# A decoder layer on one core: a new order of the first stage, weights split in halves at other places, and causal tiles that share a bank

## The reference

```
x = x + self_attention(norm(x))       # 16 heads of 32, no mask, biases on q, k, v and output
x = x + cross_attention(norm(x), ctx) # q from x; k, v from 512 latent rows of 128; causal mask
x = x + gelu(norm(x) @ p1.T + b1) @ p2.T + b2   # 2048 hidden columns
```

## Time and profile before

| | |
|---|---|
| median of 3 runs | 1316.46 us (1315.13 to 1318.9) |
| the profiled execution | 1320.07 us, of which the span of its instructions 1318.3 |
| PE busy | 1226.2 us (93%), mean granted clock 0.956 |
| DVE, ACT, POOL busy | 705.5, 468.2, 439.4 us |
| chain that ended last | PE 70%, DVE 10%, POOL 8%, DMA 4%, issue 4%, ACT 3% |

### The profile page before, as it was taken

How to read it: one execution, slowest core, us unless ns; L and a number is a source line. 1 busy time by engine, 2 the same in 40 slices (tenths; PEclk the granted TensorE clock), 3 DMA queues, 4 the chain that set the end, 5 groups by cost and what they waited for, 6 DMA issues and landing times.

```text
span 1318.3 us, 16151 instructions
## 1 busy us (share of the span) xinstructions
PE 1226.2 (93%) x6176; PEld 807.4 (61%) x6176; DVE 705.5 (54%) x1078; ACT 468.2 (36%) x832; POOL 439.4 (33%) x410
## 2 busy tenths in 40 slices
PE   3889999999999887999999999899999999999998
PEld 2644566466556533565565565455678788788786
DVE  5556667766665755566666666554344421422322
ACT  3135544444553344435435345333412111111111
POOL 5034642633464356624425425535310100100000
PEclk9798999999999978999999999975999999999999
DMA  7442222443223333325334434422032000000000
GB/s 287 124 132 77 84 80 81 106 134 81 80 80 104 104 104 104 96 81 161 95 87 139 119 88 131 136 72 80 1 95 73 33 0 1 32 0 0 32 0 32
DMA packets 42711, 110.31 MB, mean 84 GB/s; under 512 B 5520, under 2 KB 10640, under 8 KB 36496
## 3 DMA queue, kind: packets, MB, share of 16 engines
q1 hardware_dynamic: 39840, 101.99, 26.7%
q0 software_dynamic: 2080, 6.82, 1.7%
q10 hardware_dynamic: 720, 0.54, 0.1%
HBM read 71.58 MB, written 37.75 MB: 83 GB/s over the span
## 4 chain that ended last, share of the span: by engine, by line
PE 70%; DVE 10%; POOL 8%; DMA 4%; issue 4%; ACT 3%; SPq 1%; DVEq 0%; ACTq 0%; POOLq 0%
PE PS L741 14%; PE PS L742 14%; PE PS L743 14%; PE PS L859 9%; PE PS L828 7%; PE PS L845 7%; DVE m_cols L1066 5%; POOL P_sum L547 3%; DMA stackK<-scratch 2%; POOL oTL L538 2%; DMA scratch<-stage 2%; PE PS L854 1%; ACT PT L666 1%; DVE PT L1029 1%; PE PS L831 1%
## 5 line engine op out<-in xcount | busy, mean ns | idle before, releaser
L1066 DVE TENSOR_REDUCE m_cols<-PS 128x1 f32<-128x512 f32 (+3 forms) x512 | 292.9, 588 | 206.6 <-PE PS L828 102.1
L666 ACT ACTIVATE PT<-PS 128x512 f32<-128x512 f32 (+3 forms) x512 | 250.9, 516 | 216.9 <-PE PS L848 99.6
L547 POOL TENSOR_TENSOR P_sum<-PT 128x512 f32<-128x512 f32 x128 | 161.1, 1280 | 346.6 <-ACT PT L666 346.4
L828 PE MATMUL PS<-stackK,stackQ 96*128 96x512 f32 (+3 forms) x512 | 215.2, 438 | 22.0 <-DVE m_cols L1066 15.6
L845 PE MATMUL PS<-stackQ,stackK 100*128 100x512 f32 (+3 forms) x512 | 203.1, 422 | 16.5 <-ACT PT L666 15.9
L828 PEld LDWEIGHTS PS<-stackK,stackQ 96*128 96x128 f32 x512 | 105.4, 208 | 103.4 <-DVE m_cols L1066 71.4
L845 PEld LDWEIGHTS PS<-stackQ,stackK 100*128 100x128 f32 x512 | 101.3, 201 | 97.1 <-ACT PT L666 44.0
L1150 DVE CAST hidH<-hid 128x512 fp32r<-128x512 f32 x64 | 30.6, 478 | 223.3 <-ACT hid L713 221.2
L713 ACT ACTIVATE hid<-PS,b1c 128x512 f32<-128x512 f32 x64 | 43.9, 687 | 277.1 <-PE PS L743 275.2
L1073 DVE RECIPROCAL P_sum<-PS 128x512 f32<-128x512 f32 x32 | 107.4, 3358 | 58.9 <-PE PS L859 58.9
L552 POOL TENSOR_TENSOR P_sum<-P_sum,PT 128x512 f32<-128x512 f32 (+1 forms) x128 | 125.0, 1005 | 8.0 <-ACT PT L666 4.3
(11 more groups left out here) (110 smaller groups left out, 1757.9 us busy)
## 6 DMA issues: line engine op xcount, KB each, us to landing
scratch<-stage SPq DMA_DIRECT2D x128, 256.0 KB, 7.5
...
```

The lines of the kernel that those rows point to most:

```text
L547: pool.tensor_tensor(P_sum[:, h, :], PT[:, h, :], PT[:, 4 + h, :], ALU.add).then_inc(p_added, 1)
L666: nc.scalar.activation(PT[:, (4 * k + h) % 8, q0:SEQ], PS[:, T_BANK + h % 2, q0:SEQ], ACT.Exp, scale=SCALE).then_inc(p_ready, 1)
L828: mm = nc.tensor.matmul(dst[:, 0:n], stackQ[0:STACK, par, h, q * P:(q + 1) * P], stackK[0:STACK, par, h, 0:n], start=True, stop=not cross)
L1066: nc.vector.tensor_reduce(m_cols[:, q, STACK + h:STACK + h + 1], PS[:, S_BANK + q % 2, 0:keys(u, q)], AX.X, ALU.max).then_inc(s_done, 1)
```

## The change

It has four parts.

1. **First stage.** The first sequence of x is loaded in two halves, the other three as three transfers behind the stack loads of units 0 and 1 (before: one of 3 MB ahead of them). POOL makes `ident` first and the constants for the stacks later; the low parts of WQ and WO move from DVE to POOL. DVE makes its four norms in a row. The maxima of unit 0 and the pieces of K of unit 1, V tiles 2 and 3, Q and K of unit 2 form a "unit -1", whose order comes from places:

```diff
+def first_order():
+    pieces = [(what, which, k) for what, which in (("K", 1), ("V", 2), ("V", 3), ("Q", 2), ("K", 2)) for k in range(KT)]
+    work = spread(pieces[:-AFTER_TURN], *FIRST_PIECES) + [(19.0, item) for item in pieces[-AFTER_TURN:]]
+    work = [(place, *item) for place, item in work] + [(17.0, "turn", 0, 0)]
+    work += [(float(j), "max", j, 0) for j in range(len(S_FILLS[SELF]))]
```

2. **Raw tiles.** Every raw tile is 512 columns wide (a chunk is two), has its half of the buffer in turn, and a place of its own. The first two loads are issued at the end of unit 11. POOL does the tiles with a place under 3 ahead of the adds of k = 1, from 3 to 9 ahead of those of k = 2, the others behind them:

```diff
         for k in range(KT):
-            RAW.append((12, [wq2T[k * P:(k + 1) * P, :]], (WQ2, k), ("V", BATCH - 1, KT - 1)))
+            weight(FIRST_RAW, (0.7, 2.0, 8.0, 8.8)[k], wq2T[k * P:(k + 1) * P, :], WQ2, k, ("V", BATCH - 1, KT - 1))
...
+            weight(FIRST_RAW, (19.0, 20.5)[k], wkv2T[:, k * DIM:(k + 1) * DIM], WKV2, k, Q_LAST)
...
+            weight(FIRST_RAW + max(k, 1), (10.0, 14.0, 14.0, 14.0)[k], wo2T[k * P:(k + 1) * P, :], WO2, k, K_LAST)
...
+CHUNK_PLACES = [(25, (10.0, 12.0)), (26, (10.0, 12.0)), (28, (7.0, 10.0)), (28, (16.0, 20.0)), (29, (10.0, 12.0)),
+                (30, (10.0, 12.0))]
```

3. **Causal tiles.** In cross units tiles share a bank: of the scores, the two heads of a pair at k = 2 and all four at k = 3; of the tiles for maxima, all four heads at q = 0 and two at q = 1. Each head keeps its own matmul; the mask's matmul, the exponential or the maximum is one for all. Of 16 banks filled in a unit 11 are left, on either side. The adds of k = 2 take two heads at once:

```diff
+T_FILLS = {SELF: [(k, h, 1) for k in range(KT) for h in range(HPG)],
+           CROSS: [(k, h, heads) for k, heads in ((0, 1), (1, 1), (2, 2), (3, 4)) for h in range(0, HPG, heads)]}
+S_FILLS = {SELF: [(q, h, 1) for h in range(HPG) for q in range(KT)],
+           CROSS: [(q, h, heads) for q, heads in ((0, 4), (1, 2), (2, 1), (3, 1)) for h in range(0, HPG, heads)]}
...
+            for a in range(heads):
+                mm = nc.tensor.matmul(dst[:, a, :], stackK[0:STACK + HPG, par, h + a, k * P:(k + 1) * P],
+                                      stackQ[0:STACK + HPG, par, h + a, q0:SEQ], start=a == 0, stop=not cross)
```

425 lines of the change are left out of this document (220 added, 205 removed).

## The result

| | before | changed |
|---|---|---|
| executions, comparison of the prediction | 1317.68 us median (1315.13 to 1325.34) | 1251.34 and 1262.43 us |
| ratio, with 95% interval | | 0.953 (0.943 to 0.963) |
| the same pair again, on another occasion | 1319.23 us | 1261.75 us (1256.61 to 1265.79), ratio 0.9545 (0.9478 to 0.9611) |
| profiled execution (span) | 1320.07 (1318.3) | 1262.43 (1260.3) |

Two more executions of the changed kernel took 3102 and 5347 us and are left out, and that is why the pair was measured again. The change makes the kernel some 4.6% faster, and 1260 us was forecast.

The account below looks back on a forecast made before the run. Mostly plain PE work bounds the kernel, with lower clock in three stretches. Gains 15.5 + 19 + 11 + 8.5 + 3 = 57 us from 1320.1 give 1263.1 profiled, 1259.5 median, forecast 1260; range 1237 to 1283, likeliest case 1248 to 1275.

Parts of the forecast that it names:

- A: First stage up to unit 0: earlier projection and maxima, matmuls at full clock; -15.5 us.
- B: Units 12 to 15: raw tiles moved behind POOL's adds stop the PE starving in 13 to 15; -19 us.
- C: Shared banks in 16 units: 10 of 32 hand-overs a unit go, 0.7 us each unit; -11 us.
- D: Units 28 to 30: smaller or later chunks give -6 in unit 28 and -2.5 in 29 and 30; -8.5 us.
- E: DVE's statistics no longer among the maxima: 1 us in each of three cross units; -3 us, 0 to -6.
- I take 4.8 us for both together: First stage: earlier norms and WQ's low parts on POOL bring the first projection 4.8 us forward, range 3 to 6.
- the stack's wait of 1.84 us: First stage: the PE's wait for K's stack should vanish with the 3 MB transfers behind the stack loads; 1.84 us.
- The step that counted matmuls at full clock: Stretch of unit 0's maxima: 76 matmuls and four transposes at full clock take 19.5 us instead of 28.3; -8.8 us.
- the two cancel: Unit 12: k = 2 adds start later, but no tile follows them; no change from 42.76 us.
- Rival 1: Units 29 and 30: the clock stays up, 15.1 us a unit, about 1240 us in all; chance 0.22.
- Rivals 3 and 4: Shared banks expose each reading, 1357 us, chance 0.04; late raw tiles block ACT's queue, 1287 to 1290 us, chance 0.05.
- Rival 2: Half the repair: first-stage clock falls or units 13 to 15 keep half their excess, banks give nothing; 1280 to 1295, chance 0.16.

Follow-up runs that it names:

- the repeat: The changed kernel measured and profiled once more, nothing edited, against the same kernel before: 1261.75 us, ratio 0.9545.
- one_head: The changed kernel with one head in each bank again, in cross units too, and adds of one head: 1282.25 us, ratio 0.9701.
- stats_back: The changed kernel with DVE's row statistics back among the maxima (places 6 to 10): 1270.03 us, ratio 0.9608.

## Why the prediction was right, and where it was not

**The total** was right (1260 against 1251 to 1262, and 1261.75 again), and lay in the likeliest case, but it was luck in good part, since errors cancel: A and B were put 9.8 us too high (12.8 by the repeat), C, D and E 10.7 us too low.

**A, the first stage: mis-sized, -10.05 for -15.5.** The failed step is "I take 4.8 us for both together, and carry it on: everything to Q of unit 1 follows from it". The first projection came earlier than forecast (17.06 for 18.5), but nearly nothing of it reached the maxima. The port was weighed for WK's low parts beside WQ's on POOL and not for WV's beside the constants and WO's, though the same sum has "so WO costs nothing". Its reason, that POOL is idle from 42.7 to 71.0, is about another time: WO was split from 27.47 to 33.63, and WV took 8.08 us for 2.49. With that cure alone, the forecast's own numbers come out: maxima from 36.13 (forecast 36.0), first exponential 55.12 (forecast 55), unit 0's end 90.17 (106.46 - 15.5 = 91.0). That they fit so well is luck too: the 4.8 us were 6.3 to 6.5, and the stack's wait of 1.84 us did not go (1.77), since the stack came 9.8 us behind K where it had come 9.9 behind it with the 3 MB ahead. The step that counted matmuls at full clock was right at once: 18.95 us for 19.5, clock 1.00.

**B, units 12 to 15: -14.6 for -19, and only -10.6 in the repeat; right units, half the right cause.** Units 13 to 15 came out as forecast within 0.6 to 1.4 us in the first profile and within 2.1 to 2.8 in the repeat; "21 to 22 us at clock 1.00" was missed by 0.7 and by 2.0, at clock 0.93. The cause was put as the low part *between POOL's adds*, at 470.39. But the wait that was read with it ended at 469.20, before that tile; it came from the tile at the head, at 462.09, for which POOL had stood 20.88 us. Back at these places with an early high part the tiles cost nothing; what costs 9 to 12 us is POOL waiting at its head for a high part that ACT makes behind exponentials. Unit 12 was "the two cancel", within bounds of 3 worse to 4 better; it was 2.3 worse in that execution and 2.1 in the next.

**C, shared banks: 20.5 for 11.** The 0.7 a unit from hand-overs was too much for plain units: the mean of units 17 to 25 is 0.4 (0.2 in unit 17, which took 18.51 where 18.0 was forecast). Units 26 and 27 gave 5.2 together, 3.5 of them in unit 26, which splits a chunk only since the change (18.73 before, 22.04 in `one_head`, 18.50 with shared banks); why is open. The rest was counted nowhere: with shared banks the clock returns in units 29 and 30, worth 12.3.

**D, units 28 to 30: -17.4 for -8.5 and 2.1 of C.** "So the likeliest is that the clock falls again: -1.2 each" failed in its size: it does fall, but comes back some 11 us into the unit (0.83 over the unit), 20.46 us where 25 was forecast. Rival 1 (15.1 us at 1.00) was half true. Where the clock stays up, the PE's work is exactly the forecast's 15.1 us, but the unit takes 17.4, since the PE still waits for exponentials. "No raw tile is its cause as far as I see" holds for the kernel as it was: with the chunks behind the adds and one head to a bank, units 29 and 30 stayed at 26.08 and 27.09. The chunk at the head shows as a second cause only once spare work holds the clock at the start (25.04). What shortened these units was C's part. Unit 28 was forecast at 34.5 to 35 and took 36.32 at clock 0.91, and 34.24 in a run in which the clock stayed at 1.00.

**E, statistics: 8.3 for 3.** The right mechanism at the wrong size: the price is 1.7 us in unit 27 and 3.2 in units 19 and 23, where the clock falls as well, since DVE's four statistics hold up the maxima that pace the PE there. In the self units it costs nothing, as forecast.

Prices found by taking one part back out don't add up to the whole. In units 17 to 27 `one_head` costs 8.7 us and `stats_back` 8.1, together 16.7, though the whole change gave only 13.9 there, and 2.9 of these lie in units 20 and 24, which neither run touches. The parts lean on each other: moving the statistics was worth 8.1 us in units 19, 23 and 27 beside shared banks (72.47 us in `stats_back`, 64.39 in the repeat), and with one head to a bank 4.6 (71.99 before, 67.35 in `one_head`), which is nearer to the 3 of the forecast.

**Rivals 3 and 4** are out: unit 17 did not grow, and B's and D's gains came, so no late transfer cost them. One did hold ACT in unit 12 as soon as tiles were moved later (7.76 us). **Rival 2** is out too: the stretch of the maxima kept its clock (1.00), and the banks gave more than was counted.
